# One counter of units for every job, transposes of quantised weights by DMA, and loads and stores issued by the scalar engine

## The chip, the core and the metric

The kernel runs on one NeuronCore of a Trainium2 chip. The metric is device time in microseconds (us) of one execution. Three runs of the kernel before gave 928.50, 926.46 and 922.58, so the median is 926.46; the profiled execution took 926.61, of which 924.9 lie between its first and its last instruction (its span). The engines are PE (TensorE: PE is the matmul, PEld its weight load), DVE (VectorE), ACT (ScalarE), POOL (GpSimd) and SP (SyncE, which only issues DMAs). SPq, ACTq and the like are the instruction queues of these engines.

## The reference, cut to what matters

For 16 sequences of 256 tokens of width 256, with a context of the same size:

```
xn  = layernorm(x)
q   = xn @ Wq1;  k = [xn @ Wk1, ctx @ Wk2];  v = [xn @ Wv1, ctx @ Wv2]   # 8 heads of 64, 512 keys
x   = x + softmax(q k^T / 8) v @ Wo + bo
h   = layernorm(x) * gamma + beta
out = x + silu(h @ quant(sw1)^T) @ quant(sw2)^T                           # shared expert
        + p_top * silu(h @ quant(ew1[e])^T) @ quant(ew2[e])^T             # e: best of 8 experts, p_top its probability
quant(W) = scale * clip(round(W / scale), -1, 1),  scale = mean |W| of each row
```

All products are computed as sums of float16 parts (a high part, "hi", and the rest, "lo") to reach float32 accuracy. The 18 matrices to be quantised (two for each of the 8 experts and two shared ones) hold 128x1024 values each.

## The kernel before, in words

The program has three stages: a start (loads, weights split into parts), a loop over the 16 sequences, and an end, in which a table sorts all tokens by expert and 39 tiles of 128 tokens go through the routed experts. The change touches the first two and the passage to the third.

The loop is cut into **units**: one unit is one head for one block of 128 queries, 16 units to a sequence, 256 in all. In a unit, for head g:

- PE computes the scores (`scores`, L1272, two heads at a time in even units), into one of four PSUM banks S.
- DVE takes the negated maximum of each row (L1101). ACT takes exp with that bias and sums the row (L759, an ACTIVATE and a read of its accumulator). `probs` has three buffers: exp of head g waits until POOL is done with head g - 3.
- One unit later ACT rounds the probabilities to float16 (`round_probs`, L699) and POOL subtracts to get the rest (`split_probs`, L509), and SP issues one DMA that transposes both parts, 128x1024 float16 (`turn_probs`, L436). `p_split` has four buffers.
- Four units later (LAG) PE multiplies the transposed probabilities with v (`weigh_values`, L1288 to L1290, 12 short matmuls).

Beside this, each sequence has three lists of jobs, whose places stand in tables of unit numbers within a sequence:

- **Front** (`FRONT_AT`), for the next sequence: FC_CTX and FC_X transpose context and normalised x, Q0, Q1, K0 to K3 and V0 to V3 are ten products of 12 matmuls (L327; for V jobs the trace merges pairs). PE writes job j into one of two banks FB, one unit later ACT copies the hi part (`front_hi`) and DVE subtracts for the lo part (`front_lo`); a job waits until the bank, used two jobs before, has been read by DVE. The layer norm of x is: statistics on DVE, `pow` and small operations on POOL (L542 to L547), scaling on ACT (L675). Job QUANT transposes one quantised matrix on PE with eight small transposes (L1199), and ACT copies it to its place (L632).
- **Tail** (`TAIL_AT`), for the sequence before: OT0 and OT1 transpose the attention output (L1323), WO0 and WO1 multiply by Wo (L327 with TBK), then residual and layer norm (L963 to L985, POOL L567 to L573, ACT L675), HT transposes h (L1335), UP0 and UP1 are the shared expert's first product (L1344, L1345) with tanh on ACT (L731) and a product on DVE (L970), POOL scales it (L527), ACT rounds it (L692) and POOL takes the rest (L531), DOWN is the second product (L1351, L1352). All tail jobs use the one bank TBK, each after the one before has been read.
- **Weights**, one matrix for each sequence: SP loads it (L430), ACT sums the absolute values of each row (`row_sums`, L710), POOL makes scales, DVE compares with plus and minus half the scale (L850), POOL subtracts (L505).

Each engine runs its own list, written out by loops of the same form; they meet only at semaphores. The order within each engine's unit is fixed: for instance, POOL did its other jobs of a unit ahead of the unit's `split_probs`, and PE its front jobs ahead of its tail jobs. The places were chosen so that front and tail jobs of one sequence fall inside one pass of the loop over 16 units (`for b in range(-1, B + 2)`, `for u in range(16)`).

## Time and profile before

| | |
|---|---|
| median of three runs | 926.46 us |
| profiled execution | 926.61 us, span 924.9 us |
| start, until the first exp | 48.80 us |
| first sequence (16 exps) | 40.49 us |
| the next 14 sequences, together | 600.76 us |
| the last sequence, until its last exp | 35.23 us |
| from there to the end | 199.6 us |
| PE, ACT, POOL, DVE busy in the span | 77%, 75%, 66%, 66% |

The exps of ACT mark the units: the start of every sixteenth gives the boundaries in this table. Thirteen of the 14 sequences in the middle lie between 41.99 and 42.98 us, eleven of them between 42.87 and 42.89, and one took 44.10. A view by stage cuts the span at these boundaries; a view of the chain of waits follows back, from the last instruction, what released each one.

### The profile page before, as it was taken

How to read it: one execution, taken by the hardware profiler on the slowest of the kernel's cores; microseconds unless marked ns; L12 is line 12 of the kernel's file. 1: busy time of each engine (PE TensorE's matmuls, PEld its weight loads, DVE VectorE, ACT ScalarE, POOL GpSimd, SP SyncE). 2: the span in 40 equal slices, each digit the busy share in tenths (PEclk: the TensorE clock that was granted, in tenths of full speed). 3: DMA queues.
4: the chain of work that ended last, by engine and by line, in shares of the span. 5: the costliest groups of instructions: out<-in, count | busy, mean ns of one | idle time of the engine just before them, and what ended most of it. 6: DMA issues, size and time to landing. Idle time of an engine off the chain costs nothing.

```text
span 924.9 us, 22065 instructions
## 1 busy us (share of the span) xinstructions
PE 713.7 (77%) x8022; PEld 495.8 (54%) x8022; DVE 608.8 (66%) x1241; ACT 693.4 (75%) x1536; POOL 614.8 (66%) x669
## 2 busy tenths in 40 slices
PE   2768888897988788898879897889777542788883
PEld 1425656574656565565646564656554421466662
DVE  4457666675666566666657576666664239799994
ACT  5368888988888888979888978888796410588882
POOL 2146686868686867777686868686776723477773
PEclk9779999999999999999999999999998755899997
DMA  6057668686686867677877677686748400244420
GB/s 216 25 133 134 133 125 161 115 154 145 139 164 132 152 120 158 120 161 125 159 119 149 138 144 168 130 149 132 138 93 148 101 3 23 87 124 133 124 74 13
DMA packets 301980, 114.72 MB, mean 124 GB/s; under 512 B 274211, under 2 KB 291117, under 8 KB 301874
## 3 DMA queue, kind: packets, MB, share of 16 engines
q1 hardware_dynamic: 296594, 99.66, 54.9%
q0 software_dynamic: 5280, 13.64, 4.8%
q8 instruction: 66, 1.08, 0.5%
q14 instruction: 40, 0.33, 0.1%
HBM read 35.40 MB, written 13.50 MB: 53 GB/s over the span
## 4 chain that ended last, share of the span: by engine, by line
PE 30%; DVE 25%; POOL 16%; ACT 14%; issue 10%; DMA 4%; DVEq 1%; SPq 0%; ACTq 0%; POOLq 0%
PE FB L327 10%; POOL p_split L509 6%; PE TBK L327 5%; POOL g_lo L531 3%; DMA pt<-p_split 3%; DVE x L1142 3%; PE S L1272 3%; DVE gate L970 2%; DVE pt L1152 2%; DVE ot_lo L955 2%; ACT p_split L699 2%; DVE w_raw L1156 2%; POOL gate L527 2%; ACT k_st L671 2%; ACT th L731 2%
## 5 line engine op out<-in xcount | busy, mean ns | idle before, releaser
L509 POOL TENSOR_TENSOR p_split<-probs,p_split 128x512 f16<-128x512 f32 x256 | 301.7, 1183 | 77.3 <-ACT p_split L699 75.8
L759 ACT ACTIVATE probs<-S,neg_max 128x512 f32<-128x512 f32 x256 | 175.3, 685 | 15.3 <-DVE neg_max L1101 15.3
L1101 DVE TENSOR_REDUCE neg_max<-S 128x1 f32<-128x512 f32 x256 | 171.6, 677 | 8.0 <-PE S L1272 7.9
L699 ACT ACTIVATE p_split<-probs 128x512 f16<-128x512 f32 x256 | 161.2, 630 | 6.7 <-DMA pt<-p_split 1.0
L1288 PE MATMUL O<-v_st,pt 128*128 128x64 f16 x1024 | 120.7, 196 | 54.5 <-DMA pt<-p_split 49.6
L327 PE MATMUL FB<-xt_hi,w_split 128*128 128x256 f16 x768 | 144.1, 277 | 22.9 <-DVE v_st L924 11.5
L1288 PEld LDWEIGHTS O<-v_st,pt 128*128 128x128 f16 x1024 | 92.4, 99 | 120.7 <-DMA pt<-p_split 56.4
L1290 PE MATMUL O<-v_st,pt 128*128 128x64 f16 x1024 | 119.5, 195 | 0.0
L1289 PE MATMUL O<-v_st,pt 128*128 128x64 f16 x1024 | 119.4, 195 | 0.0
L1272 PE MATMUL S<-k_st,q_st 64*128 64x512 f16 x768 | 106.9, 385 | 3.1 <-ACT probs L759 3.1
L327 PE MATMUL FB<-xt_lo,w_split 128*128 128x256 f16 x384 | 106.0, 276 | 0.0
L327 PEld LDWEIGHTS FB<-xt_hi,w_split 128*128 128x128 f16 x768 | 76.1, 99 | 38.5 <-DVE k_st L932 15.9
L327 PE MATMUL FB<-w_split,xt_hi 128*128 128x512 f16 x256 | 79.1, 392 | 22.6 <-DVE xt_lo L920 22.0
L1289 PEld LDWEIGHTS O<-v_st,pt 128*128 128x128 f16 x1024 | 93.9, 99 | 1.4 <-issue 0.3
L1290 PEld LDWEIGHTS O<-v_st,pt 128*128 128x128 f16 x1024 | 94.0, 99 | 0.0
L932 DVE SCALAR_TENSOR_TENSOR k_st<-FB,k_st 128x512 f16<-128x512 f32 x64 | 44.2, 691 | 52.2 <-ACT k_st L671 52.2
L527 POOL TENSOR_TENSOR gate<-gate,up_scale 128x512 f32<-128x512 f32 x32 | 33.4, 1044 | 55.8 <-DVE gate L970 55.8
L605 POOL DMA_INDIRECT out<-row,p_split x39 | 48.7, 1249 | 24.5 <-DVE row L1165 15.0
L924 DVE SCALAR_TENSOR_TENSOR v_st<-FB,v_st 128x512 f16<-128x512 f32 x64 | 43.8, 685 | 27.6 <-ACT v_st L666 27.6
L1413 PE MATMUL S<-ht_hi,up 128*128 128x128 f16 x312 | 45.2, 229 | 21.3 <-DVE ht_lo L1137 21.3
L597 POOL DMA_INDIRECT w_split<-rows,p_split x39 | 40.9, 1049 | 24.5 <-DVE p_split L1077 13.0
L505 POOL TENSOR_TENSOR above<-above,under 128x1024 f16<-128x1024 f16 x16 | 34.0, 2123 | 31.4 <-DVE under L850 31.4
(230 smaller groups left out, 1928.8 us busy)
## 6 DMA issues: line engine op xcount, KB each, us to landing
rows<-row SPq DMA_DIRECT2D x16, 512.0 KB, 4.3
w_raw<-in_L_ffn_expert_w SPq DMA_DIRECT2D x15, 512.0 KB, 4.2
c_in<-in_ctx SPq DMA_DIRECT2D x16, 256.0 KB, 3.2
x_in<-in_x SPq DMA_DIRECT2D x16, 256.0 KB, 3.7
xb<-in_x SPq DMA_DIRECT2D x16, 256.0 KB, 3.0
pt<-p_split SPq DMA_TRANSPOSE x256, 3.1
k_st<-in_L_xattn_Wk SPq DMA_DIRECT2D x2, 512.0 KB, 8.0
w_split<-rows,p_split POOLq DMA_INDIRECT x39, 3.4
```

The source lines that it names most:

```text
L327: mm = nc.tensor.matmul(o, l, r, start=(n == 0), stop=(n == len(terms) - 1))
L509: g.tensor_tensor(p_split[n % HL_RING][:, 1, :], probs[n % PROBS_RING][:, :], p_split[n % HL_RING][:, 0, :], ALU.subtract).then_inc(p_lo_r ...
L527: g.tensor_tensor(gate[j][:, :, :], gate[j][:, :, :], sc, ALU.mult).then_inc(gated, 1)
L605: g.indirect_dma_start(out=out, out_offset=bass.IndirectOffsetOnAxis(ap=slot_idx[:, a:a + 1], axis=0), in_=e_res[a % OUTS], in_offset=None ...
L699: a_(p_split[g % HL_RING][:, 0, :], probs[g % PROBS_RING][:, :], ACT.Copy).then_inc(p_hi_ready, 1)
L759: a_(probs[g % PROBS_RING][:, :], S[u % 4][:, :], ACT.Exp, bias=neg_max[:, u % 4:u % 4 + 1], accum_out=sums[:, u:u + 1])\
L1101: v.tensor_reduce(neg_max[:, u % 4:u % 4 + 1], S[u % 4][:, :], AX.X, ALU.max, negate=True)\
L1272: last = mm(S[(u + odd) % 4][:, :], q_st[rows_, par, ql, c, tok], k_st[par][rows_, kl, c, :], start=(n == 0), stop=(n == 2))
L1288: mm(o1, pt[:, r, jb, :], v_st[par][:, 0, jb, h, :], start=(jb == 0), stop=False)
L1289: mm(o1, pt[:, r, jb, :], v_st[par][:, 1, jb, h, :], start=False, stop=False)
L1290: last = mm(o1, pt[:, r, KB + jb, :], v_st[par][:, 0, jb, h, :], start=False, stop=(jb == KB - 1))
L1413: mm(o1, w, e_hth[s][:, c, :], start=(c == 0), stop=False)
```

## The change

Every job now has one place counted in units over the whole run, relative to the first unit of its sequence (`due(n, at)` gives the sequence whose job at `at` falls on unit n), and can lie before, in or after the 16 units of the sequence's own attention. Four kinds of things change with it:

1. **Places.** The front jobs were in units 2, 4, 5, 6 to 13 and 15 of the sequence before (one more, QUANT, in 14), and now lie at -14, -13, -10 (two jobs), -8, -6, -5, -4, -2, -1, 0 and 1. The order is Q0, K0, Q1, K1, V2, V3, K2, K3, V0, V1. Tail jobs that were at 19, 20, 22, 23, 26, 29, 30 and 34 are at 18, 19, 21, 23, 29, 31, 33 and 41. Statistics of x, its POOL part and its scaling are at -17, -17 and -15 (were -16, -14, -14). On POOL `split_probs` now comes first in a unit. `normalise_heads` treats eight heads at once in place of four, and PE leaves out `weigh_values` in the unit in which that happens and does two in the next.
2. **Quantised weights.** QUANT and its two forms in the start are gone from PE and ACT. SP transposes the matrix with one DMA (`turn_ternary`), straight to its place. DVE writes its comparisons in the order of blocks that this needs. The row sums of 15 matrices move from ACT to one reduction on DVE.
3. **Who issues.** ACT issues the loads of 15 raw matrices and the stores of token rows, which were one store of 512 KB a sequence on SP, and are now two of 256 KB: h after its layer norm, the rest after the shared expert.
4. `x2` has two buffers, and each tail job has its own semaphore.

```diff
+FRONT_AT = {FC_CTX: -14, FC_X: -13, Q0: -10, K0: -10, Q1: -8, K1: -6, V2: -5, V3: -4, K2: -2, K3: -1, V0: 0, V1: 1}
+LOAD_C, LOAD_X, LOAD_RAW = -31, -27, -11
+STATS_X, RS_X, NORM_X = -17, -17, -15
+SUM_W, SCALE_W, ABOVE_W, UNDER_W, TERN_W, TURN_W = -7, -7, -5, -3, -2, -1
+OT_AT, WO_AT = (18, 21), (19, 23)
+LOAD_XB, ADD_XB, RS_H, NORM_H, STORE_H = 10, 19, 25, 27, 27
+HT_AT, HT_LO = 29, 30
+UP_AT = (31, 33)
+SCALE_G, HI_G, LO_G = (33, 34), (36, 36), (37, 39)
+DOWN_AT, ADD_R, STORE_R = 41, 45, 46
+        def due(n, at):
+            i, rest = divmod(n - at, UNITS)
+            return i if rest == 0 and 0 <= i < B else None
...
+            def turn_ternary(m, e, down):
+                sp.wait_ge(tern_ready, m + 1)
+                dst = (down16 if down else up16)[:, e, :, :].rearrange("p a (b c) -> p (a b) c", c=P)
+                sp.dma_start(dst, above[:, :], transpose=True).then_inc(tern_moved, 16)
...
-            def ternary_move(full, e, down, src, done):
-                act.wait_ge(*full)
...
-                a_(dst, src, ACT.Copy).then_inc(done, 1)
...
+            def load_raw(f):
+                act.wait_ge(tern_ready, f + 2)
+                e, down = f // 2, f % 2 == 1
+                nc.scalar.dma_start(raw_down if down else raw_up, (ew2_v if down else ew1_v)[e]).then_inc(raw_loaded, 16)
...
+                f = due(n, LOAD_RAW)
+                if f is not None and f > 0:
+                    load_raw(f)
+                t = due(n, STORE_H)
+                if t is not None:
+                    act.wait_ge(hn_ready, t + 1)
+                    nc.scalar.dma_start(rows_v[t][:, :, D:2 * D], row[:, :, D:2 * D]).then_inc(h_stored, 16)
+                t = due(n, STORE_R + 1)
+                if t is not None:
+                    act.wait_ge(r_ready, t + 1)
+                    nc.scalar.dma_start(rows_v[t][:, :, 0:D], row[:, :, 0:D]).then_inc(r_stored, 16)
...
+                        dve.wait_ge(raw_loaded, (n - 1) * 16)
+                        dve.wait_ge(half_ready, n * 3)
+                        v.tensor_reduce(w_abs[:, 0:cols], raw, AX.X, ALU.add, apply_absolute_value=True)\
+                            .then_inc(abs_ready, 1)
...
-            def transpose_ternary(n, down, dst):
...
+            for n in range(FIRST, LAST):
+                if n in PREP_AT:
+                    prep_job(PREP_AT[n])
+                for j in range(FRONT):
+                    f = due(n, FRONT_AT[j])
+                    if f is not None:
+                        front_job(f, j)
+                for g in {0: (), 1: (n - LAG - 1, n - LAG)}.get((n - LAG) % HEADS, (n - LAG,)):
+                    if 0 <= g < NU:
+                        weigh_values(g)
...
+                if n % 2 == 0 and 0 <= n + 2 < NU:
+                    scores(n + 2)
```

Two places show the move in the engines' own lists. On ACT, around the border of two sequences, before (`probs` is the exp, `p_split` the rounding, `down` the quantised matrix's copy, `under,w_abs` the row sums):

```order
L731 ACTIVATE th<-TBK,half_up 128x256 x2
L632 ACTIVATE down<-FB 128x1024
L759 ACTIVATE probs,sums<-S,neg_max 128x512
L692 ACTIVATE g_hi<-gate 128x512
L699 ACTIVATE p_split<-probs 128x512
L666 ACTIVATE v_st<-FB 128x512
L759 ACTIVATE probs,sums<-S,neg_max 128x512
L692 ACTIVATE g_hi<-gate 128x512
L699 ACTIVATE p_split<-probs 128x512
L759 ACTIVATE probs,sums<-S,neg_max 128x512
L710 ACTIVATE under,w_abs<-w_raw 128x256 x4
```

and the list of the change, from its units 14 and 15, before that border:

```order
L689 ACTIVATE ht<-TBK,gb 128x256 x2
L692 ACTIVATE ht_hi<-ht 128x512
L738 ACTIVATE probs0,sums<-S2,neg_max 128x512
L667 ACTIVATE p_split2<-probs0 128x512
L640 ACTIVATE k_st1<-FB0 128x512
L738 ACTIVATE probs1,sums<-S3,neg_max 128x512
L760 DMA rows<-row 128x2x256
L667 ACTIVATE p_split3<-probs1 128x512
L698 ACTIVATE th<-TBK,half_up 128x256 x2
L640 ACTIVATE k_st1<-FB1 128x512
L738 ACTIVATE probs2,sums<-S0,neg_max 128x512
```

The 128x1024 copy and the row sums have gone, and a DMA that ACT issues stands directly behind an exp. On SP, one sequence before (`pt` is the transposed probabilities):

```order
L450 DMA c_in<-in_ctx 128x2x256
L453 DMA x_in<-in_x 128x2x256
L436 DMA_TRANSPOSE pt<-p_split 128x8x128
L456 DMA rows<-row 128x2x512
L436 DMA_TRANSPOSE pt<-p_split 128x8x128 x4
L459 DMA xb<-in_x 128x2x256
L436 DMA_TRANSPOSE pt<-p_split 128x8x128 x4
L430 DMA w_raw<-in_L_ffn_expert_w 128x2x512
L436 DMA_TRANSPOSE pt<-p_split 128x8x128 x7
```

and in the change:

```order
L425 DMA c_in<-in_ctx 128x2x256
L418 DMA_TRANSPOSE pt<-p_split 128x8x128 x4
L429 DMA x_in<-in_x 128x2x256
L418 DMA_TRANSPOSE pt<-p_split 128x8x128 x5
L433 DMA xb<-in_x 128x2x256
L418 DMA_TRANSPOSE pt<-p_split 128x8x128 x6
L412 DMA_TRANSPOSE down<-above 128x8x128
L418 DMA_TRANSPOSE pt<-p_split 128x8x128
```

Store and raw load have left SP's list, and a seventeenth transpose of the same shape as the sixteen of the probabilities has come in behind the last but one of them.

## Rows read from the trace of the kernel before

**Rows 1.** Exps of ACT in order of time: start us, us, engine, line, operation.
```profile
48.80 0.68 ACT L759 ACTIVATE probs<-S,neg_max 128x512 f32<-128x512 f32 x1
...
432.66 0.71 ACT L759 ACTIVATE probs<-S,neg_max 128x512 f32<-128x512 f32 x1
...
725.28 0.69 ACT L759 ACTIVATE probs<-S,neg_max 128x512 f32<-128x512 f32 x1
```
**Rows 2.** Busy time by stage; columns: stretch and its us, busy us, clock, DMA, GB/s.
```profile
0.00:48.80 48.80, 26.45 (x136) 14.81 (x136) 22.41 (x38) 20.45 (x42) 8.93 (x20) 0.86 0.38 124
48.80:89.29 40.49, 29.01 (x312) 18.32 (x308) 27.50 (x54) 32.90 (x74) 22.19 (x21) 0.87 0.58 123
432.66:475.55 42.89, 36.08 (x436) 24.90 (x432) 27.82 (x57) 36.64 (x85) 31.98 (x37) 1.00 0.79 143
475.55:518.43 42.88, 35.92 (x436) 24.95 (x432) 27.81 (x57) 36.28 (x82) 31.97 (x37) 1.00 0.73 142
690.05:725.28 35.23, 23.04 (x300) 15.47 (x296) 16.39 (x35) 25.52 (x58) 25.24 (x25) 0.88 0.74 136
```
**Rows 3.** The chain of waits through one sequence: start us, us, engine, tile, line.
```profile
400.64 1.77 PE TBK L327 x24
...
402.78 0.75 PE S L1272 x6
...
420.89 1.49 PE FB L327 x12
...
431.52 1.12 POOL p_split L509
432.64 1.11 POOL g_lo L531
```
**Rows 4.** Who waited for whom in one sequence, 389.79:432.66: us, times, longest.
```profile
PE O L1288 <- DMA pt<-p_split: 2.3, 2, 2.1
...
ACT xt_hi L661 <- PE FB L1237: 1.5, 1, 1.5
```
**Rows 5.** ACT in order of time: one unit, and QUANT's copy; columns as in rows 1.
```profile
420.01 0.68 ACT L759 ACTIVATE probs<-S,neg_max 128x512 f32<-128x512 f32 x1
...
420.81 0.63 ACT L699 ACTIVATE p_split<-probs 128x512 f16<-128x512 f32 x1
421.35 0.58 ACT L671 ACTIVATE k_st<-FB 128x512 f16<-128x512 f32 x1
421.83 0.68 ACT L759 ACTIVATE probs<-S,neg_max 128x512 f32<-128x512 f32 x1
...
429.57 1.02 ACT L632 ACTIVATE down<-FB 128x1024 f16<-128x1024 f16 x1
```
**Rows 6.** DMA view of one sequence, 389.79:432.66: packets, MB, share; then us to landing.
```profile
q1 hardware_dynamic: 18241, 5.97, 73.8%
...
pt<-p_split SPq DMA_TRANSPOSE x16, 3.4
```
**Rows 7.** Groups of instructions by shape, 389.79:432.66: busy us, mean ns, idle before.
```profile
L710 ACT ACTIVATE under<-w_raw 128x512 f16<-128x512 f32 x2 | 1.2, 618 | 0.0
...
L1101 DVE TENSOR_REDUCE neg_max<-S 128x1 f32<-128x512 f32 x16 | 10.7, 676 | 0.0
...
L505 POOL TENSOR_TENSOR above<-above,under 128x1024 f16<-128x1024 f16 x1 | 2.1, 2130 | 1.2 <-DVE under L850 1.2
```
**Rows 8.** SP's queue in order of time, one transpose and one copy issued.
```profile
401.91 1.24 SPq L436 DMA_TRANSPOSE pt<-p_split  x1
403.19 0.58 SPq L456 DMA_DIRECT2D rows<-row  x1
```
**Rows 9.** The chain of waits behind the last exp; columns as in rows 3.
```profile
728.37 3.04 DMA pt<-p_split
...
732.27 0.21 PE TBK L1351
```
**Rows 10.** POOL in the start, in order of time: the second raw matrix's load.
```profile
27.18 1.02 POOL L550 DMA_DIRECT2D w_raw<-in_L_ffn_expert_w  x1 [13.56 <-DVE above L853]
```

More of the change, by code:

```diff
@@ L47 @@
 ABSENT = 8192
-FC_CTX, V2, FC_X, V3, Q0, Q1, K0, K1, K2, K3, V0, QUANT, V1 = range(13)
-FRONT_AT = {2: FC_CTX, 4: V2, 5: FC_X, 6: V3, 7: Q0, 8: Q1, 9: K0, 10: K1, 11: K2, 12: K3, 13: V0, 14: QUANT, 15: V1}
-FRONT = 13
-SPLIT = 12
-OT0, WO0, OT1, WO1, HT, UP0, UP1, DOWN = range(8)
-TAIL_AT = {3: OT0, 4: WO0, 6: OT1, 7: WO1, 10: HT, 13: UP0, 14: UP1}
-DOWN_AT = 2
-TAIL = 8
-HT_AT = next(u for u in TAIL_AT if TAIL_AT[u] == HT)
-LATE = (99,)
-NORM_X_AT = 2
-NORM_H_AT = 9
-GATE_HI_AT = {15: 0}
-SUMS_AT = 1
-QUANTISE_AT = {4: 0, 7: 1, 10: 2}
-SHARED_Q = 2
+FC_CTX, FC_X, Q0, K0, Q1, K1, V2, V3, K2, K3, V0, V1 = range(12)
+FRONT = 12
+K_JOBS = (K0, K1, K2, K3)
+V_JOBS = {V0: 0, V1: 1, V2: 2, V3: 3}
 NU = B * UNITS
@@ L143, in xattn_ffn @@
         xb = sb("xb", [P, TB, D], F32)
-        x2 = sb("x2", [P, TB, D], F32)
+        x2 = [sb(f"x2_{i}", [P, TB, D], F32) for i in range(2)]
         st2 = sb("st2", [P, TB, 6], F32)
@@ L1191, in _ @@
             pe.wait_ge(const_ready, 9)
[L1193 to L1200 removed]
             def prep_job(j):
                 at_least(pe, prep_free, j)
[L1204 to L1206 removed]
+                if j == ROUTER_W:
                     pe.wait_ge(rw_in, 16)
@@ L1378, in _, with turn_heads @@
-            slots(pe, body)
+            def turn_heads(t, i):
+                pe.wait_ge(normed, t * TB + i + 1)
+                if i == 0:
+                    at_least(pe, gate_ready, t * 2)
+                    if t == 0:
+                        pe.wait_ge(prep_free, PREP)
+                else:
+                    pe.wait_ge(x2_ready, t * 2 + 1)
+                    at_least(pe, logits_ready, t)
+                for c in range(IC):
+                    last = nc.tensor.transpose(TBK[:, c * P:(c + 1) * P], o_sb[:, i, c * P:(c + 1) * P], ident[:, :])
+                last.then_inc(ot_full, 1)
@@ new lines, in project_out, with turn_rows @@
+            def project_out(t, i):
+                pe.wait_ge(ot_lo_ready, t * 2 + i + 1)
+                if t == 0 and i == 0:
+                    pe.wait_ge(w_lo_ready, 6)
+                last = split_product(TBK[:, 0:D], [(ot_hi[:, c, :], ot_lo[:, c, :], wo_hi[:, c, :], wo_lo[:, c, :])
+                                                   for c in range(IC)])
+                if i == 0 and t > 0:
+                    last = route(TBK)
+                last.then_inc(wo_full, 1)
+            def turn_rows(t):
+                pe.wait_ge(hn_ready, t + 1)
+                pe.wait_ge(x2_ready, t * 2 + 2)
+                at_least(pe, shared_ready, t)
+                for i in range(TB):
+                    for c in range(DC):
+                        last = nc.tensor.transpose(tb2[:, c, i * P:(i + 1) * P], row[:, i, D + c * P:D + (c + 1) * P],
+                                                   ident[:, :])
+                last.then_inc(ht_full, 1)
@@ new lines, in up_shared @@
+            def up_shared(t, j):
+                if j == 0:
+                    pe.wait_ge(ht_ready, t + 1)
+                    pe.wait_ge(h_lo_ready, t + 1)
+                    if t == 0:
+                        pe.wait_ge(tern_moved, 16)
+                else:
+                    pe.wait_ge(gate_ready, t * 2 + 1)
+                for k in range(2):
+                    m = 2 * j + k
+                    for c in range(DC):
+                        w = up16[:, E, c, m * P:(m + 1) * P]
+                        mm(tb2[:, k, :], w, ht_hi[:, c, :], start=(c == 0), stop=False)
+                        last = mm(tb2[:, k, :], w, ht_lo[:, c, :], start=False, stop=(c == DC - 1))
+                last.then_inc(up_full, 1)
@@ new lines, in down_shared @@
+            def down_shared(t):
+                pe.wait_ge(g_lo_ready, t * 2 + 2)
+                if t == 0:
+                    pe.wait_ge(tern_moved, 48)
+                if t + 1 < B:
+                    pe.wait_ge(x2_ready, t * 2 + 4)
+                else:
+                    pe.wait_ge(gate_ready, t * 2 + 2)
+                for i in range(TB):
+                    tok = slice(i * P, (i + 1) * P)
+                    for c in range(FC):
+                        mm(tb2[:, i, :], g_hi[:, c, tok], down16[:, E, c, :], start=(c == 0), stop=False)
+                        last = mm(tb2[:, i, :], g_lo[:, c, tok], down16[:, E, c, :], start=False, stop=(c == FC - 1))
+                last.then_inc(down_full, 1)
```

789 lines of the change are left out of this document (348 added, 441 removed).

## The prediction

> **What bounds the kernel now.** I first cut the span at the exps of ACT, because each of the 256 units has exactly one [rows 1]. From the exp at 432.66 sixteen units later is 475.55: 42.9 us a sequence, and eleven of the fourteen sequences in the middle agree with this to 0.02 us. Such a regular beat means that a ring of waits, not chance, sets the pace. The busy time by stage says how far each engine is from being the limit of such a sequence [rows 2]: ACT is busy 36.6 and 36.3 us of 42.9, PE 36.1 and 35.9, POOL 32.0, DVE 27.8, and the 16 DMA engines 79% and 73%, about 32.6 us. Nobody is full. The loss is 6.3 us even on the busiest, and 14 such sequences are 88 us of waiting.
>
> The chain of waits shows where it comes from [rows 3]. It runs through one sequence and changes engines all the time: a Wo product on PE (1.77 us with the router), scores (0.75), a front product (1.49), and near the end of the sequence POOL's probabilities and gate rests in turn. Each change of engine happens since a result is wanted in the very unit in which it is made, while seven or eight front products stand in consecutive units and share two banks. The waits are small and many [rows 4]: 1.5 us of ACT for the transposed x, 2.3 us of PE for transposed probabilities in two places. Spreading the places attacks this ring itself; engine work hardly changes.
>
> **The work per sequence after the change.** *ACT.* Two exps in neighbouring units with one front copy between them are 1.82 us apart (420.01 to 421.83), made of 0.80 until the rounding starts, 0.54 for the rounding and 0.48 for the copy [rows 5]. A unit without a copy is thus 1.34 us. QUANT's copy leaves (1.02 us busy, 0.9 net) and so do the row sums, 1.2 us for the form with two sums and somewhat more with four and their reads of the accumulator [rows 5, 7]; I take 1.4 on average. From 36.5 us 34.2 remain. Three DMA issues come in. On SP one copy costs 0.58 us of the queue [rows 8], so ACT rises to between 34.2 (the issue runs beside the exp dispatched just before it, which lasts 0.80, and beside the layer norm) and 35.9. I take the upper end, since the store of h waits for its own layer norm and has nothing beside it.
>
> *PE.* The eight small transposes leave, about 0.5 us: 35.5. Its busy time includes modelled ends, so the true figure is lower. Two `weigh_values` in one unit after none are the same work.
>
> *DVE.* A reduction of 1024 columns comes in; the one of 512 takes 0.68 [rows 7], so at most 1.4, and four normalisations become two larger ones (nothing or a small gain): 29, not a limit. Writing the comparisons in another order of blocks I cost at nothing to 1 us; 14 us of idle time per sequence cover it.
>
> *POOL.* The same work, 32.0. The order changes: the probabilities come first, and so each transpose can start up to 1.1 us (one gate operation [rows 3]) earlier.
>
> *SP and DMA.* Per sequence the copies are 1.8 MB. In the start, where copies make nearly all the traffic, 124 GB/s over 48.8 us at a share of 0.38 is 3.06 us of all engines per MB [rows 2], so copies are 5.5 us and a transpose of probabilities is (32.6 - 5.5)/16 = 1.7 us. A seventeenth of the same shape makes 34.3 us. SP loses two copies and gains a transpose of 1.24 us of issue [rows 8]: nothing, as it idles for POOL most of the time.
>
> Here the Trainium skill speaks against the change: "VectorE: DVE Perf Modes", section The three transpose paths, puts a 128x128 transpose at 390 ns on TensorE and 1309 ns by DMA, and its rules prefer TensorE where PSUM will do. By that figure eight blocks would be an estimated 10.5 us instead of 1.7; of the 8.8 more some 3 would be slack, and the other 6, 14 times, would make the sum 917. The trace differs: a DMA of the same eight blocks lands in 3.4 us in the median, issue to end [rows 6].
>
> **The period.** The greatest of these loads is 35.9, so the period lies between 35.9 and the 42.9 of today. To choose, I walked the new places by hand with the durations above. From the tanh of UP1 in unit 2 to the copy of K1 in unit 11 ACT has nine units of 1.34, six front copies of 0.48, a tanh, two copies for OT and two gate roundings: 17.7 us, and 0.5 for the rounding ahead of K1's. PE's part begins 2.0 us later, when DVE has read UP1's bank, and holds OT0, OT1, WO0 with the router (1.77), WO1, four pairs of scores (0.75 each), four products of 1.3 (one is 1.49 with its first wait [rows 3]), one FC job, DOWN and eight `weigh_values` of 0.36: 17.2 us. PE arrives at 19.2 where ACT is ready at 18.2, so ACT waits 1.0 us there. In the other seven units PE has 15 us and ACT 18, and no other wait of ACT comes out. I add 0.4 for hand-overs and loads that meet transposes: 35.9 + 1.0 + 0.4 = **37.3 us**. The fourteen sequences then take 522.2 instead of 600.8: **-78.6**.
>
> A transpose of probabilities may take its time: POOL is done about 1.65 us into the unit after the exp, PE wants the result some 3.5 units (8.2 us) after that unit's start, so 6.5 us are there for what lands in 3.4 now [rows 6]. A raw load that gets in between from ACT's queue adds at most its own 1.6 us (0.5 MB at 3.06).
>
> **Start, last sequence, end.** Start and first sequence take 89.3 us. V0, V1 and the transposes of two quantised matrices no longer stand ahead of the first exps, and the statistics of x no longer wait behind a weight. Against it the third raw matrix is still loaded by POOL only after the second is quantised (the first such load is issued at 27.18, 13.56 us after POOL fell idle [rows 10]), and ACT's row sums stand in line for it. I take **-7**, between 0 and -13. The last sequence has no front work; ACT is busy 25.5 of its 35.2 [rows 2]; I take **-3.5**, between 0 and -5. Behind the last exp the chain waits 3.04 us for the last transpose, then DOWN of sequence 14 runs 16 matmuls 0.215 apart [rows 9], 3.4 us, ahead of OT0 of sequence 15. Now OT0, WO0 lie ahead and DOWN behind; but UP0 comes ahead of the router's last product. Net **-4.7**, between -8 and 0. The expert stage is untouched.
>
> Sum, against the profiled execution: 926.6 - 78.6 - 7 - 3.5 - 4.7 = 832.8, **833 us**. That execution is within 0.2 us of the median of the three runs, so no correction is due.
>
> **Rivals.** *(A) A smaller ring closes.* POOL has in units 14 and 15 the rest of h (1.1), the weights' subtraction (2.1 [rows 7]) and the pow chain of x (1.6) around a single split of probabilities, and exps can run ahead of POOL by three heads. If exp waits there, or DVE's unit 4 with four jobs makes it wait, 2.8 us a sequence come back: period 40.1, 872 us; with both it may reach 905. For it: the ring of today is made of just such pieces. Against: two units of ACT before and after give 4.7 us of slack. *(B) The ring stays.* Some wait that I missed ties a sequence as now, the places move and the period does not: 926.6 less the 15.2 of start and end, 911 us, or 925 with a 1 us longer wait. Against: every producer I went through lies one or more units further from its reader. *(C) Slower: transposes become the bound.* Copies from ACT's queue no longer queue behind SP's transposes but run among them, and there is one transpose more. If one costs 2.35 us of the DMA engines in place of 1.7, a sequence needs 17 x 2.35 + 5.5 = 45.5 us: 926.6 + 14 x 2.6 - 15.2 = 948 us. It decides from 17 s + 5.5 > 42.9, s = 2.2 us. The DMA share of 79% speaks for it; against, copies are among the transposes today as well, and PE waits for them only 2.3 us a sequence [rows 4]. The page quoted above, whose figure for a block is well over what I worked out, lies on this side. *(D) Better.* All three issues of ACT are hidden and PE's true load is lower: period 35, 801 us.
>
> **Numbers.** Forecast 0.68 (806 to 868), A 0.14 (868 to 905), B 0.06 (900 to 930, half of it under 917), C 0.08, D 0.04. Less than 1% of the time (9 us) cannot be told from no change. Faster by more than that: 0.68 + 0.14 + 0.04 + 0.02 = 0.88; within it 0.04; slower 0.08. The range 806 to 890 leaves out D (0.04), the top of A (0.02), B and C (0.14): 0.20.
>
> **What would show it.** Exps sixteen units apart should be 37 us apart, ACT busy for 34 to 36 of them, without the 1.02 us copy; the largest wait of ACT should be for a K1 or another product of units 8 to 11. DMA share should rise to about 0.9 of a shorter sequence, transposes should land within 6 us in the median, and PE should seldom wait for them. The first exp should start near 40 us. A is right if exp waits for POOL's p_split or DVE's neg_max; B if the period is still near 42.9; C if transposes take 5 us and more in the median and PE waits for them in every second unit. The forecast is wrong above all if issuing a DMA costs ACT far more than SP's 0.58 us: at 2.5 us each the period would be 43.

## The result, and the profile of the changed kernel

The changed kernel takes 847.18 us in the median of four runs (844.60 to 850.77), the kernel before 926.06 on the same chip (four runs, 922.58 to 928.50). The ratio is 0.915, with a 95% interval from 0.910 to 0.921. The prediction was 833 us, in a range from 806 to 890.

The profiled execution took 850.77 us, 848.8 of it span. Its exps cut it as [rows 1] cut the one before. First the exps of ACT in order of time; columns are start us, us, engine, line, operation.

```profile
45.27 0.68 ACT L738 ACTIVATE probs<-S,neg_max 128x512 f32<-128x512 f32 x1
...
88.77 0.68 ACT L738 ACTIVATE probs<-S,neg_max 128x512 f32<-128x512 f32 x1
...
469.88 0.70 ACT L738 ACTIVATE probs<-S,neg_max 128x512 f32<-128x512 f32 x1
...
653.74 0.67 ACT L738 ACTIVATE probs<-S,neg_max 128x512 f32<-128x512 f32 x1
```

The view by stage answers to [rows 2]. Columns are the stretch and its length, busy us of PE, PEld, DVE, ACT and POOL with the number of instructions, the granted clock, the DMA share and GB/s.

```profile
0.00:45.27 45.27, 22.20 (x106) 12.79 (x107) 21.51 (x41) 16.86 (x38) 5.88 (x23) 0.85 0.39 128
45.27:88.77 43.50, 31.48 (x301) 19.23 (x300) 28.93 (x47) 30.00 (x68) 25.52 (x24) 0.80 0.70 134
393.10:431.44 38.34, 35.03 (x429) 24.94 (x427) 28.60 (x55) 34.10 (x77) 33.85 (x37) 1.00 0.87 166
431.44:469.88 38.44, 35.10 (x429) 25.16 (x427) 29.31 (x55) 34.00 (x77) 33.25 (x37) 1.00 0.90 165
621.86:653.74 31.88, 22.63 (x313) 15.56 (x310) 17.80 (x36) 26.28 (x60) 26.91 (x27) 0.91 0.84 158
653.74:848.80 195.06, 123.88 (x1260) 93.62 (x1260) 153.60 (x317) 105.99 (x223) 115.10 (x104) 0.86 0.26 74
```

| stage | before | predicted | after |
|---|---|---|---|
| start and first sequence | 89.3 | 82 | 88.8 |
| the 14 sequences in the middle | 600.8 | 522.2 | 533.1 |
| one of them, in the mean | 42.9 | 37.3 | 38.1 |
| last sequence | 35.2 | 31.7 | 31.9 |
| behind the last exp | 199.6 | 194.9 | 195.1 |

So the gain of 76 us in the span is 67.7 in the middle, 0.5 in the start with the first sequence, 3.4 in the last sequence and 4.6 in the end. The regular beat of [rows 1] is gone: sequences now differ (36.20 to 38.58, and one of 41.82, as one of before took 44.10). The loss of 6.3 us a sequence on the busiest engine has become 3.3 on PE (38.4 less 35.1) and 4.4 on ACT, whose busy time does not count the DMAs that it issues.

The waits of one sequence, 393.10:431.44, answer to [rows 4]. Columns are who waited, on whom, us in total, times, the longest.

```profile
POOL p_split L490 <- ACT p_split L667: 3.5, 5, 1.4
...
PE O L1239 <- DMA pt<-p_split: 2.0, 2, 1.0
...
PE TBK L1269 <- DVE gate L924: 1.3, 1, 1.3
...
ACT p_split L667 <- DMA pt<-p_split: 1.0, 1, 1.0
```

PE waits for transposed probabilities 2.0 us in all as against 2.3, the longest 1.0 as against 2.1; ACT's wait for the transposed x is gone. What ACT does wait for is a p_split buffer whose transpose hasn't landed, and K1, the one wait that the prediction worked out (1.0 us). ACT in order of time:

```profile
417.86 0.60 ACT L640 ACTIVATE k_st<-FB 128x512 f16<-128x512 f32 x1 [0.88 <-PE FB L311]
```

The chain of waits of the same sequence changes engines far less than [rows 3]; its columns are start us, us, engine, tile, line.

```profile
399.88 1.00 POOL gate L508
400.88 1.11 POOL p_split L490
...
403.23 1.13 POOL p_split L490
404.38 1.60 SPq L418
...
406.03 0.57 SPq L429
...
406.70 6.29 DMA pt<-p_split
...
413.07 0.64 ACT p_split L667
...
413.78 1.16 POOL p_split L490
```

POOL is back to back from unit 15 to unit 3. Then SP issues, the transpose of 406.70 lands after 6.29 us, ACT rounds into the buffer that it frees, and POOL splits again. The DMA view of this sequence (packets, MB, share of 16 engines; then the median us to landing) shows the second queue that transposes now share the engines with; it answers to [rows 6].

```profile
q1 hardware_dynamic: 18768, 5.25, 76.6%
q10 hardware_dynamic: 1072, 1.05, 9.9%
...
pt<-p_split SPq DMA_TRANSPOSE x16, 3.8
```

### The profile page after: what moved, and what is told of

The parts are those of the page before. It is cut to its first block, busy times and chain, and to the rows that moved or that the text cites. A ratio compares the mean times of both kernels' runs of the same rounds, so it can differ in the third digit from the quotient of the medians.

```text
span 848.8 us, 21620 instructions
## 1 busy us (share of the span) xinstructions
PE 689.4 (81%) x7878; PEld 490.4 (58%) x7878; DVE 623.5 (73%) x1188; ACT 654.1 (77%) x1430; POOL 635.0 (75%) x673
## 4 chain that ended last, share of the span: by engine, by line
POOL 26%; DVE 18%; PE 15%; ACT 14%; DMA 14%; issue 8%; SPq 1%; DVEq 1%; ACTq 1%; POOLq 0%
POOL p_split L490 14%; DMA pt<-p_split 12%; PE FB L311 5%; ACT probs L738 4%; DVE x L1106 3%; POOL above L486 3%; ACT p_split L667 2%; DVE pt L1116 2%; DVE w_raw L1120 2%; POOL gate L508 2%; POOL ht_lo L532 2%; DVE o_sb L1112 2%; POOL row L528 1%; ACT v_st L635 1%; PE S L1223 1%
## 5 line engine op out<-in xcount | busy, mean ns | idle before, releaser
L490 POOL TENSOR_TENSOR p_split<-probs,p_split 128x512 f16<-128x512 f32 x256 | 323.4, 1269 | 77.8 <-ACT p_split L667 76.2
L311 PE MATMUL FB<-xt_hi,w_split 128*128 128x256 f16 x768 | 145.8, 281 | 8.9 <-DVE xt_lo L875 6.2
L1239 PE MATMUL O<-v_st,pt 128*128 128x64 f16 x1024 | 117.5, 196 | 27.0 <-DMA pt<-p_split 26.8
L1240 PE MATMUL O<-v_st,pt 128*128 128x64 f16 x1024 | 116.8, 195 | 0.0
L1241 PE MATMUL O<-v_st,pt 128*128 128x64 f16 x1024 | 116.8, 195 | 0.0
L311 PE MATMUL FB<-xt_lo,w_split 128*128 128x256 f16 x384 | 107.9, 281 | 0.0
L591 POOL DMA_INDIRECT out<-row,p_split x39 | 48.7, 1248 | 24.9 <-DVE row L1129 15.5
L924 DVE SCALAR_TENSOR_TENSOR gate<-th,TBK 128x512 f32<-128x512 f32 x32 | 22.0, 687 | 57.6 <-ACT th L698 57.6
L1392 PE MATMUL S<-ht_hi,up 128*128 128x128 f16 x312 | 45.1, 229 | 21.7 <-DVE ht_lo L1101 21.7
L640 ACT ACTIVATE k_st<-FB 128x512 f16<-128x512 f32 x64 | 37.7, 590 | 18.4 <-PE FB L311 18.4
```

What stands on the lines that cost most here:

```text
L311: mm = nc.tensor.matmul(o, l, r, start=(n == 0), stop=(n == len(terms) - 1))
L490: g.tensor_tensor(p_split[n % HL_RING][:, 1, :], probs[n % PROBS_RING][:, :], p_split[n % HL_RING][:, 0, :], ALU.subtract).then_inc(p_lo_r ...
L591: g.indirect_dma_start(out=out, out_offset=bass.IndirectOffsetOnAxis(ap=slot_idx[:, a:a + 1], axis=0), in_=e_res[a % OUTS], in_offset=None ...
L1239: mm(o1, pt[:, r, jb, :], v_st[par][:, 0, jb, h, :], start=(jb == 0), stop=False)
L1240: mm(o1, pt[:, r, jb, :], v_st[par][:, 1, jb, h, :], start=False, stop=False)
L1241: last = mm(o1, pt[:, r, KB + jb, :], v_st[par][:, 0, jb, h, :], start=False, stop=(jb == KB - 1))
```

## The experiments

The chips differ. Four chips ran the experiments, and on three of them (all but e12's) the kernel before takes 948 to 952 us in place of 926, and the stage behind the last exp takes 209 to 234 us in place of 195. On one of these chips alone it took 208.8 us in e8 and 226.1 in e5, so the times there carry a spread that the sequences do not have. The sequences take the same time everywhere: for the same changed kernel 37.96 on one of them and 38.08 here. So each experiment is read by its exps first, and by its ratio to the kernel before on its own chip second. "Period" is the mean of the 14 sequences in the middle of the one profiled execution; two executions of the same kernel differ by 0.12.

| kernel | first exp | first sequence | period | time | ratio (95% interval) |
|---|---|---|---|---|---|
| before | 48.8 | 40.5 | 42.9 | 926.1 | 1 |
| changed | 45.3 | 43.5 | 38.08 | 847.2 | 0.915 (0.910 to 0.921) |
| e5, changed again | 43.5 | 43.4 | 37.96 | 877.2 | 0.922 (0.915 to 0.929) |
| e1, three issues on SP | 44.7 | 43.6 | 37.21 | 858.9 | 0.905 (0.900 to 0.909) |
| e7, raw load on SP | 45.1 | 42.9 | 37.62 | 873.6 | 0.922 (0.914 to 0.929) |
| e3, copy back on ACT | 44.8 | 44.3 | 37.96 | 877.6 | 0.926 (0.921 to 0.930) |
| e4, six split buffers | 45.6 | 43.3 | 37.74 | 873.0 | 0.919 (0.912 to 0.925) |
| e8, ternary on DVE | 44.5 | 42.5 | 37.71 | 864.3 | 0.915 (0.907 to 0.924) |
| e11, second transpose | 43.6 | 41.5 | 37.99 | 884.0 | 0.931 (0.924 to 0.938) |
| e2, places of before | 50.2 | 41.6 | 46.44 | 1007.4 | 1.061 (1.053 to 1.068) |
| e6, and order of before | 50.0 | 42.3 | 47.20 | 1023.0 | 1.080 (1.072 to 1.088) |
| e9, all places of before | 48.7 | 44.3 | 45.34 | 999.4 | 1.046 (1.033 to 1.059) |
| e10, all that helped | 44.2 | 35.3 | 37.16 | 864.7 | 0.911 (0.906 to 0.916) |
| e12, OT a unit later | 45.1 | 36.2 | 40.30 | 873.9 | 0.943 (0.941 to 0.945) |

**Part 3 undone: who issues the copies.**

```
-  ACT: load_raw(f) at LOAD_RAW; store of h at STORE_H; store of the residual at STORE_R + 1
+  SP, ahead of the unit's transposes: load_raw(f) at LOAD_RAW; stores at STORE_H + 1 and STORE_R + 1
```

> The three copies a sequence that ACT issues (raw weights, store of h, store of the residual) are issued by SP, in the same units; all else as in the changed kernel (847.2 us). Theory of the prediction: each issue costs ACT the 0.58 us that SP needs for one, so 3 x 0.58 x 14 = 24 us come back: 823 us. My theory since the trace of the changed kernel: the issues lie beside running activations (ACT busy 34.1 of 38.3, not 35.9) and the ring goes through POOL and the transposes, so ACT gains next to nothing: 843 to 851 us. Rival: SP now waits for h, for the residual and for the ternary matrix ahead of a transpose that PE wants, and each sequence grows by 0.5 to 1 us: 854 to 861 us.

None of the three held: the period fell by 0.8 us, to 37.21. One sequence of it in the view by stage:

```profile
385.55:422.34 36.79, 35.00 (x429) 24.91 (x427) 29.11 (x55) 34.05 (x77) 33.55 (x37) 1.00 0.93 173
```

ACT is busy 34.1 us with and without the issues, but this says nothing of their cost, since busy time does not count them. Its rows in order of time do. In all 15 cases the issue of a raw load runs beside an exp, as here, and the store of the residual runs in the same way beside a rounding:

```profile
405.63 0.69 ACT L738 ACTIVATE probs<-S,neg_max 128x512 f32<-128x512 f32 x1 [0.72 <-DVE neg_max L1045]
405.64 0.38 ACTq L704 DMA_DIRECT2D w_raw<-in_L_ffn_expert_w  x1
```

The store of h is different. It waits until ACT's own layer norm has ended (at 420.10), its issue then stands alone, and the rounding behind it starts 1.61 us after the layer norm did:

```profile
419.02 1.08 ACT L644 ACTIVATE row<-x,shift,rs 128x256 f32<-128x256 f32 x2
420.13 0.40 ACTq L756 DMA_DIRECT2D rows<-row  x1
420.63 0.63 ACT L667 ACTIVATE p_split<-probs 128x512 f16<-128x512 f32 x1 [0.53 <-ACT row L644]
```

In e1 the same rounding starts 0.98 us after the layer norm (410.56 and 411.54), so this one issue costs ACT 0.6 us and the other two nothing that the rows show. And in the waits PE loses 3.3 us to transposes that have not landed in two sequences of the changed kernel, 1.6 in two of e1. The Trainium skill, "DMA: Bandwidth & Descriptors", section Issuing engines are not separate DMA queues, says that copies of several engines run on the same 16 DMA engines and interleave, and that only issue time is saved. The trace agrees: the two queues share the 16 engines (76.6% and 9.9% in the DMA view above), and nothing was gained by taking the issues from SP. To tell ACT's wait from the queue, one of the three went back alone:

```
-  ACT: load_raw(f) at LOAD_RAW
+  SP, ahead of the unit's transposes: load_raw(f) at LOAD_RAW
```

> Only the raw weight load goes back to SP; ACT keeps both stores of rows. With all three on SP the period was 37.2 in place of 38.1. If the copies of another queue among the transposes cost it (a raw load is 0.5 MB of the 1 MB), half or more comes back here: period 37.4 to 37.7. If it is ACT's wait for its own layer norm ahead of the store of h (0.53 us), nothing does: 38.0 to 38.2.

The period is 37.62, inside the range of the first theory: 0.34 to 0.46 of the 0.75 to 0.87 us came back with half of the bytes, and ACT's gap of 0.5 behind its layer norm is still there. So the queue that copies run on has a price. The other half went back in e1 with the two stores, which are the other half of the bytes and, with the store of h, the gap as well; no run tells these two apart. The time, 873.6 against 877.2 for the changed kernel on the same chip, is too near to decide anything by itself.

**The changed kernel on another chip.** No edit.

> The changed kernel once more, as the measure for the others on this chip. The first four experiments ran on a chip on which the stage behind the last exp took 220 to 224 us in place of 195, while sixteen exps took the same time as before. If the chip makes that, the period is 38.1 here again, and the end is 195 or 220 as it is for the kernel before.

The period is 37.96, the end 226 us: the sequences are the same on both chips, and the end is not.

**Part 2: the load taken from ACT, and the transpose given to DMA.**

```
+  f = due(n, -1)                       # ACT, unit 15
+  if f is not None and f > 0:
+      a_(moved, w_hi[:, WQ], ACT.Copy)  # 128x1024 f16
```

> ACT gets back a copy of 1024 columns in unit 15 of each sequence (what it evicted there for the weights before; here of constant weights into a buffer that nobody reads), about 1.0 us busy and 0.9 net. Prediction's rule, period = load of ACT + its one wait: +0.9 x 14 = 12.6, 860 us. My theory, the ring is POOL and the transposes with ACT idle 4 us a sequence: 0 to +4, 847 to 851 us. It decides whether the removed copy was worth anything by itself.

```profile
393.46:431.39 37.93, 34.88 (x428) 25.01 (x426) 28.42 (x55) 34.93 (x77) 33.45 (x37) 1.00 0.89 168
```

The view by stage has ACT busy 34.93 in place of 34.05 us, and the period does not move (37.96). The load of ACT doesn't set the pace of the changed kernel, and in it such a copy costs nothing. What the copy cost in the kernel before, and what the row sums and the eight small transposes of PE are worth, no run shows. The other side of that trade:

```
   turn_ternary(f + 2, f // 2, f % 2 == 1)
+  sp.dma_start(moved, above, transpose=True).then_inc(tern_moved, 16)
```

> The changed kernel with the weights' transpose by DMA done twice in each sequence, the second time into a buffer that nobody reads. The prediction priced one at 1.7 us of the 16 engines, hidden. Prediction: DMA share from 0.88 to 0.91, period 38.0 to 38.3, time within 4 us of the changed kernel (ratio 0.915 to 0.925). Rival, DMA bound: +1.7 a sequence, +24 us, ratio 0.94 or more.

The period is 37.99, so an eighteenth transpose is as good as free, although the DMA share reads 0.90 and 0.95 in two sequences (0.87 and 0.90 in two of the changed kernel). The ratio, 0.931, is above the range given; its end, in which no weights are transposed, took 230 us. The 10.5 us for eight blocks that the prediction estimated from "VectorE: DVE Perf Modes" of the Trainium skill would not fit, as time of all 16 engines, into the 4 us a sequence that they had left; the rise of the share is 1 to 2 us and speaks for the 1.7.

**The ring through POOL.** Two edits loosened it.

```
-HL_RING = 4
+HL_RING = 6
```

> Six p_split buffers in place of four, nothing else: the rounding on ACT no longer waits for the transpose of four heads earlier (2.5 us of waits in two sequences, the longest 1.6). Theory: the buffers close the ring through POOL, SP, the transpose and back to ACT; with two more ACT runs further ahead and the period falls by 0.5 to 1.2 us: 830 to 840 us. Rival: the three buffers of exps or PE's own wait for the transposed probabilities take its place at once: 845 to 849 us.

ACT's waits for a p_split buffer are gone, and its waits for neg_max rise from 1.2 to 2.9 us in two sequences: the period is 37.74, the rival nearer to the truth than the theory. Nearly all of the 0.2 to 0.3 is the one long sequence, 38.5 here and 41.8 in the changed kernel. The mean of the other thirteen is 37.68 here, 37.79 in the changed kernel and 37.67 in e5, so two more buffers gain at most 0.1 there. The long sequence is also absent from e11, which has four buffers (its longest is 39.4), so it can't be put down to them with certainty.

```
   POOL: - ternary(f + 2) at TERN_W
   DVE:  + v.tensor_tensor(above, above, under, ALU.subtract) at TERN_W
```

> The subtraction that makes the ternary matrix (POOL 2.12 us, in unit 14 of each sequence) is done by DVE in the same unit; in the start DVE does the same in 0.70. Theory: POOL, busy 33.5 of 38.3 and back to back from unit 15 to 3, is the core of the ring, so the period falls by 0.8 to 2 us: 36.1 to 37.3, ratio to before 0.89 to 0.905. Rival: POOL's load is covered and only the transposes and PE count: 37.9 to 38.2, no change.

The period is 37.71, between the two (37.50 without the long sequence, 40.4 here, against 37.67 to 37.79). The subtraction was not the 0.70 us that DVE takes for it in the start. DVE in order of time, then POOL:

```profile
420.20 1.68 DVE L839 TENSOR_TENSOR above<-above,under 128x1024 f16<-128x1024 f16 x1
```
```profile
420.07 1.27 POOL L528 TENSOR_TENSOR row<-row,x 128x512 f32<-128x512 f32 x1
421.29 1.61 POOL L490 TENSOR_TENSOR p_split<-probs,p_split 128x512 f16<-128x512 f32 x1
```

DVE starts while POOL adds, ends 0.54 us after POOL's operation does, and POOL's next split, 1.16 us in the median, takes 1.61. The 1.68 is also the median of all sequences. Neither operation seems to run while the other does: the row sets 1.0 us of waiting before DVE's 0.69, and 0.45 before POOL's 1.16. The Trainium skill, "SBUF — State Buffer", section SBUF: two separate sides, names it: a VectorE operation with two inputs in SBUF and a GpSimd operation that reads SBUF take a shared pair of ports as an exclusive lock. The trace agrees, and of the 2.1 us that left POOL 0.45 came back in this one split.

**Part 1 undone: the places.** This is the part that I held to be nearly all of the gain, and it took three runs. (The tables of places also carry a few that go with them and are left out here.)

```
-FRONT_AT = {FC_CTX: -14, FC_X: -13, Q0: -10, K0: -10, Q1: -8, K1: -6, V2: -5, V3: -4, K2: -2, K3: -1, V0: 0, V1: 1}
+FRONT_AT = {FC_CTX: -14, V2: -12, FC_X: -11, V3: -10, Q0: -9, Q1: -8, K0: -7, K1: -6, K2: -5, K3: -4, V0: -3, V1: -1}
-OT_AT, WO_AT = (18, 21), (19, 23);  HT_AT, HT_LO = 29, 30;  UP_AT = (31, 33);  DOWN_AT = 41
+OT_AT, WO_AT = (19, 22), (20, 23);  HT_AT, HT_LO = 26, 28;  UP_AT = (29, 30);  DOWN_AT = 34
-SCALE_G, HI_G, LO_G = (33, 34), (36, 36), (37, 39)
+SCALE_G, HI_G, LO_G = (30, 31), (31, 32), (32, 33)
```

> Part 1 undone alone: the front products stand in the consecutive units of before (context transposed at -14, V2 -12, x -11, V3 -10, then one product a unit to -3, V1 at -1), the tail at its old distances (OT 19 and 22, WO 20 and 23, HT 26, UP 29 and 30, DOWN 34 with its gate steps), the weights' transpose by DMA and ACT's three issues stay as changed. Theory: the places made most of the gain, so exps sixteen units apart return to 41.5 to 42.9 us: 847 + 14 x (42.2 - 38.1) = 904 us, between 896 and 916. Rival: the lighter ACT (34.1 against 36.5 us) made half of it, then the period is 40.2 and the time 875 us or less.

Then, on top of this, the order within a unit:

```
   POOL: - split_probs first in the unit      + last in the unit
   PE:   - front job, then weigh_values, DOWN + weigh_values, DOWN, then front job
```

> The places of before, and with them its order within a unit: POOL's split of the probabilities last in the unit, PE's weighing of values and DOWN ahead of the front product. Parts 2 and 3 stay. With the places alone the period was 46.4 us, longer than the 42.9 of before: there DOWN waits for POOL's g_lo, which the split ahead of it delays. Theory: order and places belong together, the period is 42 to 43, and the time is that of the changed kernel + 14 x 4.4 = 62 us, ratio to before 0.97 to 1.00. Rival: the ring lies in the copies of ACT's queue or in the merged normalisation of eight heads; then it stays near 46 and the ratio is 1.04 or more.

And on top of both the steps of x and of the weights:

```
-STATS_X, RS_X, NORM_X = -17, -17, -15
+STATS_X, RS_X, NORM_X = -16, -14, -14
-LOAD_RAW = -11;  SUM_W, SCALE_W, ABOVE_W, UNDER_W, TERN_W, TURN_W = -7, -7, -5, -3, -2, -1
+LOAD_RAW = -14;  SUM_W, SCALE_W, ABOVE_W, UNDER_W, TERN_W, TURN_W = -11, -10, -8, -6, -5, -4
```

> As the experiment with places and order of before (period 47.2), and now also the steps that it had left at their new places go to where they were or near: statistics of x in unit 0, its pow chain on POOL and its normalisation in unit 2 (they stood in 15 and 1), the loads of context and x in unit 4, the ternary subtraction in unit 11 (it stood in 14), the weights' other steps three or four units earlier. Theory: POOL had its ternary step, the pow chain and two gate scalings together just ahead of the g_lo on which DOWN waits; without that lump the old ring alone is left: period 42 to 43.5, ratio to before 0.98 to 1.01, and then the places are what the change gained by. Rival: it stays above 45; then something else of the change (one normalisation for eight heads, two weighings in one unit) costs more than 3 us a sequence and the new places hide it.

The periods are 46.4, 47.2 and 45.3, all longer than the 42.9 of before. In each of them ACT, DVE and POOL do the same work as in the changed kernel to within 1.5 us and PE to within 2.4, which is its lower clock (0.93 in e2 and e6), and the only thing moved is where in the sequence it stands; this costs 7 to 9 us a sequence, more than the 4.8 that the whole change gained. So the places are needed, but taking them back does not bring back the kernel before: e9's own rival, that something else of the change costs time at the old places and the new ones hide it, is what its 45.3 shows. The sum of e2's expectation (904 us) was too low by some 80, once the 25 us of its chip are taken off, and that order and places belong together, as I thought for e6, was wrong: the order made it worse by 0.8. The lump on POOL was real. In e2 the chain of waits reads:

```profile
464.06 0.72 POOL rs L546
...
465.04 1.11 POOL p_split L490
466.15 1.11 POOL g_lo L512
467.26 1.11 POOL p_split L490
468.37 1.12 POOL g_lo L512
```

e9 takes the pow chain out from ahead of the two g_lo, among the other steps that it moves, and gains 1.9 us.

What is left against before is 2.4 us. PE's clock suggests itself. DOWN follows a wait for a transpose, and here its sixteen matmuls take 3.05 us, with the granted clock at the lower level (1.2 GHz, matmuls 0.21 apart), while one sequence later they take 1.91 at the upper one (2.4 GHz, 0.11 apart), behind a wait that is no shorter:

```profile
459.46 0.24 PE L1241 MATMUL O<-v_st,pt 128*128 128x64 f16 x1 [2.05 <-DMA pt<-p_split]
...
460.09 0.40 PE L1318 MATMUL TBK<-down,g_hi 128*128 128x256 f16 x1
...
462.87 0.27 PE L1319 MATMUL TBK<-down,g_lo 128*128 128x256 f16 x1
...
505.10 0.20 PE L1241 MATMUL O<-v_st,pt 128*128 128x64 f16 x1 [2.17 <-DMA pt<-p_split]
...
507.10 0.27 PE L1319 MATMUL TBK<-down,g_lo 128*128 128x256 f16 x1
```

But the period does not follow the clock. Two sequences of e9, the first with a DOWN of 2.86 us, the second with that of 1.9, in the view by stage:

```profile
180.86:226.19 45.33, 37.30 (x428) 25.42 (x426) 28.66 (x56) 34.34 (x77) 32.47 (x37) 0.96 0.71 140
501.18:546.53 45.35, 35.80 (x428) 24.57 (x426) 28.63 (x56) 34.34 (x77) 32.42 (x37) 1.00 0.69 140
```

The kernel before is alike: DOWN takes 1.9 us in seven and 3.1 to 3.5 in six of its middle sequences, and most of both kinds last 42.88. So DOWN's clock is not what makes the period of either. The chain of waits through 501.18:546.53 names another candidate, two operations of DVE that do not stand in the chain of 432.66:475.55 in the kernel before:

```profile
515.89 1.21 DVE w_abs L832
...
525.52 1.21 DVE above L841
```

The first is the row sums, which the change moved from ACT to DVE; the second is the first comparison, which e9 has in unit 8 and the kernel before had in unit 7, off its chain. The exps around them are 4.55 and 4.28 us apart, 3.42 and 3.00 in the kernel before. Together they are the size of the 2.4, but this is a reading of one chain: no run took them away, nor the merged normalisation of eight heads and the two weighings in one unit.

**One place alone.** The last run came from a row of the waits: PE stood 1.3 us ahead of OT0 in every sequence.

```
-OT_AT, WO_AT = (18, 21), (19, 23)
+OT_AT, WO_AT = (19, 22), (20, 23)
```

> The version with all that helped (period 37.16), and the tail's first transposes of o and their product one unit later: OT at 19 and 22, WO at 20 and 23 in place of 18 and 21, 19 and 23. In every sequence PE stood 1.3 us ahead of OT0, since DVE reads UP1's bank for the gate in that very unit; that wait should go. Theory, a wait of the fullest engine (35.0 of 37.2) is worth its length if nothing else is late there: period 36.0 to 36.6, time 8 to 16 us under that version, ratio to before 0.895 to 0.905. Rival: WO1 now follows OT1 by one unit in place of two, so PE waits there for DVE's ot_lo, or the transposes by DMA (share 0.92) are the floor: 36.9 to 37.4, no change.

The wait went and the period rose by 3.1 us, to 40.30. The waits of one sequence:

```profile
DVE ot_lo L903 <- ACT ot_hi L698: 3.4, 1, 3.4
...
PE TBK L311 <- DVE ot_lo L903: 2.4, 2, 2.2
ACT ot_hi L698 <- PE TBK L1270: 1.8, 1, 1.8
```

OT0's rest now falls into DVE's unit 4, where the normalisation of eight heads stands ahead of it, and PE waits 2.2 us for it with the next scores queued behind; OT1 and WO1 follow each other in neighbouring units, and ACT waits 1.8 us at OT1's copy. The same engines, the same work, three jobs one unit later: this is the plainest sign of how much hangs on the places, and that a wait seen in a trace is not worth its length.

**What helped, together.** e10 is e1, e4 and e8 in one, and a step for the start, which the trace of the changed kernel had asked for. POOL there, in order of time:

```profile
44.93 2.12 POOL L486 TENSOR_TENSOR above<-above,under 128x1024 f16<-128x1024 f16 x1
47.36 0.84 POOL L571 DMA_DIRECT2D w_raw<-in_L_ffn_shared_w  x1 [0.31 <-POOL above L486]
```

The third raw matrix is issued after the pow chain of x and the subtraction, though its buffer had been free since DVE's second comparison (41.09 to 42.30). In unit 1 ACT's row sums wait for it, with all later exps queued behind them:

```profile
53.42 0.63 ACT L678 ACTIVATE under<-w_raw 128x512 f16<-128x512 f32 x1 [6.24 <-DMA w_raw<-in_L_ffn_shared_w]
```

```
   POOL, unit -1:
+  pool.wait_ge(sign_ready, 4); g.dma_start(out=raw_down, in_=sw2)     # first in the unit
   ... pow chain of x ...
   ternary(1)
-  pool.wait_ge(tern_ready, 2); g.dma_start(out=raw_down, in_=sw2)
```

> A version that may beat the changed kernel, of four edits: the three copies issued by SP (period 37.2 in place of 38.0), the ternary subtraction on DVE (37.7), six split buffers (37.7), and in the start POOL issues the third raw load as soon as the second matrix's comparisons are done, not after x's pow chain and its own ternary step (the changed kernel issued it at 47.06, the comparisons ended at 42.31). Theory, one ring with slack spread thin: the gains add in part, period 36.3 to 36.9, and the first sequence falls from 43.4 to 39 to 41; against the changed kernel 14 x 1.4 + 3 = 23 us less, ratio to before 0.89 to 0.90. Rival, DMA engines are the floor (share 0.93 with the copies on SP): period 37.0 to 37.3 and only the start gains, ratio 0.90 to 0.91.

```profile
41.54 0.75 POOL L534 DMA_DIRECT2D w_raw<-in_L_ffn_shared_w  x1 [10.39 <-DVE under L837]
```

POOL's issue above is the third raw matrix, now 5.8 us earlier. The next two rows are the first sequence and one of the middle, columns as in the view by stage:

```profile
44.19:79.47 35.28, 27.98 (x301) 17.34 (x300) 29.28 (x48) 29.72 (x68) 22.93 (x23) 0.95 0.86 158
414.23:451.38 37.15, 34.96 (x425) 24.93 (x424) 31.15 (x56) 34.21 (x76) 32.05 (x36) 1.00 0.91 171
```

The first sequence falls from 43.4 to 35.3 us, twice what I expected: the 6.2 us of wait are gone, and the clock of this stretch is 0.95 in place of 0.80. The other three edits alone left it between 42.5 and 43.6. The period is 37.16, no better than e1's 37.21: the small gains don't add. The last exp stands at 629.4 us in place of 650.4 (e5), and the time is 864.7 against 884.0 for e11 on the same chip, whose last exp is at 650.9 like that of the changed kernel. So e10 is about 19 us or 2% better than the changed kernel; on a chip where the end takes 195 us it should come to some 826 us (629.4 + 195.1 + 2), an estimate.

## Why the prediction was right, and where it was not

**The mechanism** was right, and B (the period stays near 42.9) and C's whole price (948 us) fell with it: the ring of waits between engines was the loss, the places broke it, and work per engine barely moved. Undone, it costs all of the gain and more (e2, e6, e9), while a copy's load on ACT (e3) and one more transpose by DMA (e11) are worth nothing in the changed kernel. What the places would gain in the kernel before, without the other parts, no run shows, and the 2.4 us by which e9 is slower than before say that the other parts have a price that the new places hide.

**The last sequence and the end** came out to 0.2 us (31.9 and 195.1). For the end the mechanism is seen too: OT0 of the last sequence starts 6.8 us behind the last exp (660.54) in place of 11.2 (736.46), 4.4 of the 4.6 us gained.

**Start and first sequence** is the term that was mis-sized: 88.8 us in place of 82. I had named the reason (the third raw matrix waits for the second, ACT's row sums stand in line), and given it a bound of 0 for the term, but chose -7. The first exp came 3.5 us earlier, not 8.8: POOL issued the second matrix at 31.3, later than the 27.18 of [rows 10], and ACT waited 10.2 us for it; the first sequence got 3.0 longer, with the 6.24 above in it. e10, which removes that wait beside its other edits, shortens the first sequence by 8.1 us.

**The period**: 38.1, not 37.3, 10.9 us in all, of which some 4.0 are the one long sequence (41.82, the others 37.79 in the mean). The number was near, but its composition was not: I had let ACT's load of 35.9 set it, 34.2 of work and 1.7 for three issues. The work is 34.1, as worked out. The step "I take the upper end" failed: two issues run beside an operation and only the store of h stands alone, as I had said of it, so that the three cost 0.6 and not 1.7. And the load doesn't set the period at all: 0.9 us more changes nothing (e3). Against that, the wait for K1 came as worked out, 0.88 us in place of 1.0. What I left out was the ring through p_split's four buffers and the latency of transposes, with POOL full for five units ahead of it: a part of rival A. Six buffers bring back at most 0.1 a sequence outside the long one (e4), since the next wait takes their place. A part of C was true as well, transposes that copies of another queue make late; with the gap behind ACT's layer norm it is 0.8 to 0.9 (e1), as large as the whole miss of 0.8. That the forecast of 37.3 still came near is in part luck: an issue cost that was too high by 1.1 stood in for waits that I had left out. POOL's order, split first, which I had said starts a transpose up to 1.1 us earlier, no run took back alone.

**The chances**: half of B's 0.06 lies under 917 us, which is 0.03 and not the 0.02 of the sum; the chance of a gain of more than 1% comes to 0.89.

**DMA**: a share of 0.87 to 0.90 against 0.9, a landing of 3.8 us in the median of this sequence and 3.4 over the whole span. "PE should seldom wait for them" was right (twice in a sequence).

## What to carry to other kernels

When no engine is full, ask of each result in which unit it is made and in which it is wanted, and change the places as a set; a single place moved by one unit, to remove a visible wait, cost 3 us of 37. A load taken from the busiest engine is worth nothing until something shows that this engine sets the pace: give it the load back and see. An issue of a DMA cost its engine nothing here while it ran beside another operation; one that had to wait for its own engine's result cost 0.6 us, and moving the bytes to another queue than the transposes' cost about as much. And when an edit is taken back, look at the other parts at the old places too: e9 is slower than the kernel before although its jobs stand nearly where they stood.

## What the runs showed of the hardware that I had not expected

- A copy's issue on ACT's queue takes 0.37 to 0.47 us and can run beside an activation; SP's queue shows 0.58 for one [rows 8], and 0.57 in the median for the loads of x in the changed kernel.
- The same subtraction of 128x1024 float16 takes DVE 0.69 us in the start and 1.68 beside POOL (e8), and it stretches POOL's next operation from 1.16 to 1.61.
- The granted clock differs between sequences of the same work, 0.96 in some and 1.00 in others (e9, before). DOWN took 1.9 us at the upper level behind a wait of 2.17 us and 3.05 mostly at the lower behind one of 2.05, and sequences of either kind last 45.3 us.
- The expert stage takes 195 to 196 us on two chips and 209 to 234 on three others, whatever the version. Single instructions of ACT and DVE last the same to within 2% (DVE's 128x512 product 680 and 689 ns), POOL's do not (its stores of rows 1248 ns in the changed kernel, 1089 in e5), and the waits between engines are longer (POOL ahead of these stores 56.7 us in e5, 24.9 in the changed kernel). What makes these waits stays open.
